# Two dense mixtures of experts in a vision tower: down products in three fp32r parts with tokens along the columns, and router products and convolution taps moved

## The reference, cut to what matters

```python
# f0: every expert on every token, gates from a tree of sigmoids
h = jnp.einsum('nd,edh->neh', flat_x, w1) + b1[None]     # 8 experts, hidden 512
h = jax.nn.gelu(h, approximate=False)
y = jnp.einsum('neh,ehd->ned', h, w2) + b2[None]
out = jnp.einsum('ned,ne->nd', y, leaf_probs)
# f2: the same form, hidden 256, gelu with tanh, gates = the two best of a softmax
# state layer: four taps of a convolution over the tokens, then a scan
yc = sum((conv_w[None, :, k:k + 1] * xp[:, :, k:k + S] for k in range(D_CONV)))
```

## Time and profile before

| | |
|---|---|
| median of the runs | 1373.87 us |
| the profiled execution, its own time | 1372.67 us |
| its span | 1370.9 us |
| PE busy | 1214.8 us (89%) |
| DVE, ACT, POOL busy | 740.2, 749.8, 465.4 us |
| down products, L367, both mixtures | 1728 instructions, 208.4 us busy |
| up products, L352 | 720 instructions, 169.5 us |
| gelus, L380 | 240 instructions, 148.4 us |
| mean granted TensorE clock | 0.933 |

### The profile page before, as it was taken

The page is one execution under the profiler, slowest core; times in us unless marked ns, Lnnn a source line. Parts: engine busy times, 40 slices in busy tenths (PEclk is TensorE's granted clock), DMA queues, the critical chain, the costliest instruction groups (busy, mean ns, idle before and its releaser), DMA issues. The chain is left out here.

```text
span 1370.9 us, 32149 instructions
## 1 busy us (share of the span) xinstructions
PE 1214.8 (89%) x9999; PEld 1041.0 (76%) x9999; DVE 740.2 (54%) x2665; ACT 749.8 (55%) x2598; POOL 465.4 (34%) x844
## 2 busy tenths in 40 slices
PE   8999989999998999868287599998999899868996
PEld 5777779999997888758176477787999687647885
DVE  0588721111115489935655587863332388744774
ACT  1588734444443455427244488864434298743995
POOL 0488730010003268846177243221000011022552
PEclk9999979999999799979599799988999899968998
DMA  6100000010001000000411300000000000023441
GB/s 264 53 2 3 2 1 16 17 32 15 16 0 47 1 1 2 2 16 21 164 47 38 118 1 2 2 2 8 16 15 8 12 2 0 1 72 89 137 139 57
DMA packets 39495, 49.33 MB, mean 36 GB/s; under 512 B 8181, under 2 KB 27492, under 8 KB 39116
## 3 DMA queue, kind: packets, MB, share of 16 engines
q1 hardware_dynamic: 33500, 36.28, 8.6%
q0 software_dynamic: 4176, 6.56, 1.8%
q10 hardware_dynamic: 1696, 4.98, 0.9%
HBM read 41.78 MB, written 6.56 MB: 35 GB/s over the span
## 5 line engine op out<-in xcount | busy, mean ns | idle before, releaser
L380 ACT ACTIVATE f_hid<-quad_bank,f_b1s 128x512 f32<-128x512 f32 (+1 forms) x240 | 148.4, 645 | 176.8 <-PE quad_bank L352 176.5
L470 DVE SCALAR_TENSOR_TENSOR XT<-bank,GATE,XT 128x128 f32<-128x128 f32 x288 | 81.0, 344 | 244.9 <-PE bank L367 244.6
L367 PEld LDWEIGHTS bank<-f_w2s,f_hid 128*128 128x128 f32 x1728 | 206.3, 196 | 3.8
L367 PE MATMUL bank<-f_w2s,f_hid 128*128 128x128 f32 x1728 | 208.4, 279 | 0.0
L352 PE MATMUL quad_bank<-XP,f_w1p 128*128 128x512 f32 (+1 forms) x720 | 169.5, 383 | 0.0
L352 PEld LDWEIGHTS quad_bank<-XP,f_w1p 128*128 128x128 f32 x720 | 125.3, 193 | 21.2
L810 ACT ACTIVATE a_E<-quad_bank,a_shift 108x108 f32<-108x108 f32 x352 | 118.8, 356 | 3.3 <-DVE a_shift L877 2.8
L301 POOL TENSOR_TENSOR f_w1p<-f_w1s,const 128x512 fp32r<-128x512 f32 (+1 forms) x16 | 13.3, 829 | 221.2 <-DMA f_w1s<-in_f_w 221.2
L66 PE MATMUL quad_bank<-const 128*128 128x256 f32 x212 | 62.5, 453 | 15.4 <-PEq L2101 4.5
L810 ACT ACTIVATION_READ_ACCUMULATOR a_E<-quad_bank,a_shift 108x1 f32 x352 | 74.5, 212 | 0.0
L612 POOL TENSOR_TENSOR a_ve<-a_mv,const 108x1 f32<-108x1 f32 x44 | 8.4, 192 | 182.0 <-DVE a_mv L934 181.4
(11 more groups left out here) (455 smaller groups left out, 2959.3 us busy)
## 6 DMA issues: line engine op xcount, KB each, us to landing
a_wqk<-in_a_wqk SPq DMA_DIRECT2D x24, 256.0 KB, 2.6
pats<-in_patches SPq DMA_DIRECT2D x5, 648.0 KB, 10.9
pats<-in_patches ACTq DMA_DIRECT2D x5, 648.0 KB, 12.6
a_wo<-in_a_wo SPq DMA_DIRECT2D x24, 128.0 KB, 2.0
f_w1s<-in_f_w SPq DMA_DIRECT2D x8, 256.0 KB, 2.7
f_w2s<-in_f_w SPq DMA_DIRECT2D x8, 256.0 KB, 3.1
f_w1a<-in_f_w SPq DMA_DIRECT2D x1, 2048.0 KB, 10.4
f_w2a<-in_f_w SPq DMA_DIRECT2D x1, 2048.0 KB, 15.5
```

The lines of the kernel that those rows point to most:

```text
L367: mm = pe.matmul(self.y_bank(n)[:, g * D:(g + 1) * D], self.hid[:, n % 2, c, g * 128:(g + 1) * 128], self.w2s[:, u, c * 128:(c + 1) * 128] ...
L380: act.activation(self.hid[:, n % 2, c, 0:k * 128], self.m.quad_bank[:, i % 4, 0:k * 128], self.func, bias=self.b1s[:, u, c:c + 1]).then_in ...
L470: ins = dve.scalar_tensor_tensor(out=h, in0=y[:, (g - c0) * D:(g - c0 + 1) * D], scalar=m.GATE[:, bass.ds(e + g * 8, 1)], in1=h, op0=ALU.m ...
```

## The change

- `down` has the weights stationary and 512 tokens as columns: per chunk the high and the low weight part times the high hidden part (L458), and after all chunks the high weight part times the low hidden part (L463): 12 fp32r products per block in f0, 6 in f2, with channels on partitions in one bank.
- ACT copies each gelu's f32 result to a high part (`gelu_high`), DVE subtracts for the low part (`lows`). POOL splits the down weights too. In f2 the ups run two blocks ahead (`lead`), in f0 one.
- Gates are turned once (in block 2 of expert 0), stored to DRAM, and for each expert and block loaded again with every partition holding the same row (`repeat`, 256 KB, four buffers). DVE computes (y + b2) * gate (`gated`) and adds (`add`); expert 0's sum is kept raw and multiplied when its gates are there (`raw`, `lazy`). The sums have channels on partitions, so behind the last down only the turning back is left, of which three parts stand between the last downs.
- `route` makes two products per tile, of 16 and 8 columns, one tile per attention step; the best-of-softmax gates come in two pieces behind `raw` of blocks 0 and 1. The loops over experts are written out.
- The taps are loaded early in a0 and made by POOL behind f0's last weight split (`Taps`); the first convolution input is made by ACT and DVE, and PE's first convolutions stand between turns and routes.

```diff
+    def sync(self, sp):
+        sp.dma_start(self.win[:, :], self.io["ss_win"]).then_inc(self.loaded, 16)
+        sp.dma_start(self.raw, self.io["ss_taps"]).then_inc(self.loaded, 16)
...
+    def gpsimd(self, pool):
+        pool.wait_ge(self.loaded, 32)
+        one = self.m.one.broadcast_to([128, 512])
+        for k in range(TAPS):
+            pool.tensor_tensor(self.raw[:, k, :], self.raw[:, k, :], self.win[:, CW:CW + 512], ALU.mult).then_inc(self.steps, 1)
+            pool.wait_ge(self.steps, 2 * k + 1)
+            pool.tensor_tensor(self.wtp[:, 0, k, :], self.raw[:, k, :], one, ALU.mult).then_inc(self.steps, 1)
+            pool.wait_ge(self.steps, 2 * k + 2)
+            pool.tensor_tensor(self.wtp[:, 1, k, :], self.raw[:, k, :], self.wtp[:, 0, k, :], ALU.subtract).then_inc(self.made, 1)
...
+        def repeat(e, n):
+            k = self.gate_at(e, n)
+            if k >= 4:
+                sp.wait_ge(*self.gate_used(k - 4))
+            _, _, t0, w = self.block(e * self.nb + n)
+            sp.dma_start(self.gb[:, k % 4, 0:w], self.g_rows[e:e + 1, t0:t0 + w].broadcast_to([128, w])).then_inc(self.g_loaded[k % 4], 16)
...
+        sp.wait_ge(self.gt_ready, 1)
+        for k in range(2):
+            sp.dma_start(self.g_rows[4 * k:4 * k + 4, :].rearrange("e (t k) -> (e t) k", k=128), self.gT[:, k, :]).then_inc(self.g_stored, 16)
+        sp.wait_ge(self.g_stored, 32)
+        load(2)
+        for n in range(self.nb):
+            repeat(0, n)
+            repeat(1, n)
+        for e in range(2, self.experts):
+            if e + 1 < self.experts:
+                load(e + 1)
+            for n in range(self.nb):
+                repeat(e, n)
...
+    def split_down(self, pool, e):
+        pool.wait_ge(self.w_loaded[1], (e + 1) * 16)
+        if e > 1:
+            pool.wait_ge(self.y_psum, (e - 1) * self.nb)
+        self.split(pool, e, 1)
+    def split(self, pool, e, k):
+        high, low = self.wp[k][:, e % 2, 0, :], self.wp[k][:, e % 2, 1, :]
+        pool.tensor_tensor(high, self.ws[k][:, :], self.m.one.broadcast_to([128, self.chunks * 128]), ALU.mult).then_inc(self.w_high[k], 1)
+        pool.wait_ge(self.w_high[k], e + 1)
+        pool.tensor_tensor(low, self.ws[k][:, :], high, ALU.subtract).then_inc(self.w_split[k], 1)
...
+            out = psum[:, (t - base) * 16:(t - base + 1) * 16]
+            pe.matmul(out, self.xp[:, 0, t * 128:(t + 1) * 128], self.wrp[:, :, :].rearrange("p a e -> p (a e)"), start=True, stop=False,
+                      skip_group_check=True)
+            mm = pe.matmul(out[:, 0:8], self.xp[:, 1, t * 128:(t + 1) * 128], self.wrp[:, 0, :], start=False, stop=True,
+                           skip_group_check=True)
...
+        at_least(pe, self.y_used, i - 1)
+        for c in range(self.chunks):
+            q = i * self.chunks + c
+            pe.wait_ge(self.hid_high, q + 1)
+            for a in range(2):
+                pe.matmul(self.y_bank(i)[:, 0:w], self.wp[1][:, e % 2, a, c * 128:(c + 1) * 128], self.hi[:, q % self.ring, 0:w],
+                          start=(c == 0 and a == 0), stop=False)
+        for c in range(self.chunks):
+            q = i * self.chunks + c
+            pe.wait_ge(self.hid_low, q + 1)
+            mm = pe.matmul(self.y_bank(i)[:, 0:w], self.wp[1][:, e % 2, 0, c * 128:(c + 1) * 128], self.lo[:, q % self.ring, 0:w],
+                           start=False, stop=(c == self.chunks - 1))
+        mm.then_inc(self.y_psum, 1)
...
-        pe.wait_ge(self.hid_ready, e * (self.nb * self.chunks) + (n + 1) * self.chunks)
-        if n == 0:
-            at_least(pe, self.y_used, e * self.nb + 1)
-        elif n > 1:
-            pe.wait_ge(self.y_used, e * self.nb + n)
-        for g in range(k):
-            for c in range(self.chunks):
-                mm = pe.matmul(self.y_bank(n)[:, g * D:(g + 1) * D], self.hid[:, n % 2, c, g * 128:(g + 1) * 128],
-                               self.w2s[:, u, c * 128:(c + 1) * 128], start=(c == 0), stop=(c == self.chunks - 1))
-        mm.then_inc(self.y_psum, 1)
...
+    def gelu_high(self, act, i, c):
+        e, n, t0, w = self.block(i)
+        q = i * self.chunks + c
+        act.wait_ge(self.hid_full, q + 1)
+        at_least(act, self.y_psum, i - self.lead)
+        act.activation(self.hi[:, q % self.ring, 0:w], self.full[:, q % 4, 0:w], ACT.Copy).then_inc(self.hid_high, 1)
+    def hidden(self, act, i):
+        for c in range(self.chunks):
+            self.gelu(act, i, c)
+            if c:
+                self.gelu_high(act, i, c - 1)
+        self.gelu_high(act, i, self.chunks - 1)
...
+    def lows(self, dve, i):
+        e, n, t0, w = self.block(i)
+        for c in range(self.chunks):
+            q = i * self.chunks + c
+            dve.wait_ge(self.hid_high, q + 1)
+            at_least(dve, self.y_psum, i - self.lead)
+            dve.tensor_tensor(self.lo[:, q % self.ring, 0:w], self.full[:, q % 4, 0:w], self.hi[:, q % self.ring, 0:w],
+                              ALU.subtract).then_inc(self.hid_low, 1)
...
+    def lazy(self, dve, n):
+        _, _, t0, w = self.block(n)
+        k = self.take_gates(dve, 0, n)
+        dve.wait_ge(self.y_used, n + 1)
+        x = self.sums[:, t0:t0 + w]
+        dve.tensor_tensor(x, x, self.gb[:, k % 4, 0:w], ALU.mult).then_inc(self.lazied, 1)
+    def gated(self, dve, i):
+        e, n, t0, w = self.block(i)
+        k = self.take_gates(dve, e, n)
+        dve.wait_ge(self.y_psum, i + 1)
+        if i - 2 >= self.nb:
+            dve.wait_ge(self.summed, i - 2 - self.nb + 1)
+        dve.scalar_tensor_tensor(out=self.gated_y[:, i % 2, 0:w], in0=self.y_bank(i)[:, 0:w], scalar=self.b2s[:, e:e + 1],
+                                 in1=self.gb[:, k % 4, 0:w], op0=ALU.add, op1=ALU.mult).then_inc(self.y_used, 1)
+    def add(self, dve, i):
+        e, n, t0, w = self.block(i)
+        dve.wait_ge(self.y_used, i + 1)
+        if e == 1:
+            dve.wait_ge(self.lazied, n + 1)
+        else:
+            dve.wait_ge(self.summed, i - 2 * self.nb + 1)
+        x = self.sums[:, t0:t0 + w]
+        dve.tensor_tensor(x, x, self.gated_y[:, i % 2, 0:w], ALU.add).then_inc(self.summed, 1)
...
+        for i in range(downs, self.last):
+            if ups <= i + self.lead < self.last:
+                self.up(pe, i + self.lead)
+            self.down(pe, i)
+            if i == 2:
+                turn_gates()
+            if i == nb - 1 and self.aside is not None:
+                pe.wait_ge(self.gt_ready, 1)
+                self.aside.tensor(pe)
+            if i > self.last - nb:
+                back(i - (self.last - nb) - 1)
+        for j in range(nb - 1, len(CHUNKS)):
+            back(j)
...
+        for i in range(self.last):
+            e, n = divmod(i, nb)
+            if done <= i + self.lead < self.last:
+                self.lows(dve, i + self.lead)
+            if e == 0:
+                self.raw(dve, n)
+                if n < len(self.gates_last):
+                    self.gates_last[n](dve)
+                if n == len(self.gates_last) - 1:
+                    dve.drain()
+                    dve.tensor_copy(self.gs[:, :, :].rearrange("p e t -> p t e"), m.GATE[:, :].rearrange("p (t e) -> p t e", e=8)).then_inc(self.gs_ready, 1)
+                continue
...
             def after_step(t):
-                if t == G + 2:
-                    mix.route(pe, 0, 8, qkbank[0])
                 if t == G + 3:
-                    mix.route(pe, 8, 14, qkbank[0])
                     pe.wait_ge(exps, 2 * G)
-                    mix.up(pe, 0, 0, 0)
-                if t == G + 4:
-                    mix.up(pe, 0, 0, 1)
+                    pe.wait_ge(mix.lg_ready, 1)
+                    mix.up(pe, 0)
                 if t == G + 5:
-                    mix.route(pe, 14, 16, qkbank[0])
-                    mix.down(pe, 0, 0, 0, 0)
+                    mix.route(pe, early_tiles, 14, qkbank[0], early_tiles)
+                    mix.up(pe, 1)
                 if t == G + 6:
-                    mix.up(pe, 0, 0, 2)
+                    mix.route(pe, 14, 16, qkbank[0], early_tiles)
+                    mix.down(pe, 0)
                 if t == G + 7:
-                    mix.route(pe, 16, NT, qkbank[0])
+                    mix.route(pe, 16, NT, qkbank[0], early_tiles)
             run(pe, step, depth)
             if mix is not None:
-                mix.down(pe, 0, 0, 0, 1)
-                for n in range(3, mix.nb):
-                    mix.up(pe, 0, 0, n)
-                    mix.down(pe, 0, 0, 0, n - 1)
-                mix.down(pe, 0, 0, 0, mix.nb - 1)
-                mix.tensor(pe)
+                mix.tensor(pe, 2, 1)
...
-            keep_busy(pe, m, seg_bank, 10)
-            pe.wait_ge(r_loaded, 16)
-            for n, (c, k) in enumerate(CHUNKS):
-                keep_busy(pe, m, seg_bank, 1)
-                if n:
-                    route(n - 1)
-            route(nb - 1).then_inc(lg_psum, 1)
-            pe.wait_ge(taps_split, 1)
```

(33 more changed lines are left out.)

729 lines of the change are left out of this document (274 added, 455 removed).

## The result

| | before | after |
|---|---|---|
| median of the runs | 1374.04 us | 1312.31 us (1310.78 to 1315.38) |
| the profiled execution | 1372.67 us, span 1370.9 | 1315.38 us, span 1313.6 |
| down products, both mixtures | 208.4 us busy | 178.8 us (L458 115.0, L463 63.8) |

What follows compares the result with a forecast made beforehand. PE was taken to set the pace in f0. Gains of 19.4, 8, 21.8, 7.2 and 8.1 us less a 1.1 loss made 63.4 off the profiled 1372.67: 1309.3, median 1310.5 us, range 1298 to 1332.

Steps and rivals of the forecast that it cites:

- main term: Down blocks in f0 fall from 3.48 to an up block's 2.84 us, giving steady f0's 19.4 us gain.
- page rule: TensorE price: three one-pass parts cost three quarters of f32, 2.61 us a block; total near 1297; rejected for the rows.
- steady f0: f0 from block 3's up in expert 0 to the last down's end: 212.7 to 193.3 us, gain 19.4.
- POOL makes them beside the last two experts: Making the convolution's taps on POOL late in f0, rather than on DVE, was to cost nothing.
- f0's start: Fewer router products and a shorter stretch to block 3's up in f0: gain 8 us, bounds 0 and 12.
- tails: Stretch behind the last down in f0 and f2: gain 10.9 us each, 21.8 in all, bounds 8 and 12 each.
- state phase: From its first statistics to the scan's first transposes: 38.55 to 31.3 us, gain 7.2, bounds 3 and 11.
- f2's start: Gain 5.6 us from routers and clock, loss 6.7 around the gates' turn: net loss 1.1; bounds gain 6, loss 5.
- f2 steady: f2's remaining experts to the last down's end, at 13.0 us each: 100.4 to 92.3 us, gain 8.1.
- first rival: DVE and POOL never overlap, so an f2 expert takes 15.4 us; total 1327 us; chance 0.13.
- The sign that the forecast gave for this rival: DVE's lows and POOL's splits longer than 0.68 and 0.73 us, or PE waiting for low parts in f2.
- second rival: Repeated gates arrive late from DRAM in both mixtures, costing 81 us in all; total 1391 us; chance 0.05.

Runs made afterwards that it cites:

- e5: Changed kernel with both mixtures' down products in true f32 at 512 columns, other engines' work kept; 1361.8 us, ratio 0.9735 to the kernel before.
- e10: e8 with POOL's taps in four pieces behind the splits of experts 2 to 5 instead of one burst; 1301.2 us, ratio 0.9493 to the kernel before.
- e7: Changed kernel with the convolution's taps made by DVE at the state phase's start instead of POOL; 1333.7 us, ratio 0.9540 to the kernel before.
- e2: Changed kernel with POOL's splits of expert 1's weights moved into the attention's steps; 1354.1 us, ratio 0.9575 to the kernel before.
- e8: Changed kernel with expert 1's splits where POOL waits and f2's gates turned behind the fourth down; 1332.0 us, ratio 0.9526 to the kernel before.
- e3: Changed kernel with f0's early up and down products issued sooner, beneath the hand-overs; 1342.1 us, ratio 0.9599 to the kernel before.
- e1: Changed kernel, unedited, run again on another chip; 1349.6 us, ratio 0.9652 to the kernel before.
- e4: Changed kernel with f2's gates turned behind the fourth down block instead of the third; 1333.3 us, ratio 0.9538 to the kernel before.
- e12: Changed kernel, unedited, run beside e9 and e10 on the same chip; 1313.2 us, ratio 0.9589 to the kernel before.
- e6: Changed kernel with the downs' third product (low weights by high hidden values) left out; 1313.0 us, ratio 0.9389 to the kernel before.
- e9: Changed kernel with every load of repeated gates issued twice, the second into unread spare buffers; 1321.1 us, ratio 0.9636 to the kernel before.

## Why the prediction was right, and where its steps were not

**The main term was right in cause and, for a block, in size.** A down block at an up block's price, 2.84, measured 2.80. e5 shows that it is the parts that count: with f32 and 512 columns the block is back at 3.44. The page rule weighed there (the Trainium skill, FP8 and Floating Point Precision, TensorE Precision Notes: four passes for true FP32) would have three parts at three quarters, an estimate; on this chip 2.78 against 3.44 is 0.81, so the rows were the better price.

**That steady f0 gained 18.9 for 19.4 is partly luck.** Up and down take 5.58 us for the forecast's 5.68, so an expert takes 25.05 for 25.7, some 4.5 us less in seven experts. The step "POOL makes them beside the last two experts ...: nothing" was false and took them back: the burst of taps stretches the last two distances to 28.5 and 27.3 us (the last is 25.9 in e10), and costs 4.0 us by e7 and 4.4 by e10.

**f0's start: the term was mis-sized, 8 forecast and 1.7 measured.** From the first up to block 3's the forecast had 24.1 us, the trace has 30.07. First up and output product take 5.4 for 3.9, the stretch from there to the last router product 17.0 for "about 14.5, with the second up and the first down beneath them", the up and down behind it 7.7 for 5.7.

The last of these is explained: 1.9 us are the wait for ACT, of which the forecast had nothing. Expert 1's splits held the low parts up (5.53 us for four), and with them the logits, the gates' table change and the gelus. In e2 and e8, where they don't meet, the start is 2.2 us shorter. The other 4 us lie in the hand-overs, with PE's waits of 2.2 and 4.0 us and the low clock of the second up behind them. It is tempting to blame PE's order, in which the second up stands behind a hand-over; but e3 put it ahead of that, another hand-over got longer, and the start lost 1.6. So the chain through DVE, POOL, PE and ACT is itself longer than forecast, and why stays open.

Another 2 us belong to this one execution: its two slices of 5 us from 55 to 65 us, in the attention, have a granted clock of 0.61 and 0.70, where the kernel before and e1, e4 and e12 have 1.00, and its first up starts at 173.31. In the other traces but e2's it starts at 170.3 to 171.7, and block 3's up in the unedited ones at 200.6 and 200.7: 4.5 us gained of the 8, against the one trace of before.

**The tails** were right (10.8 and 10.6 for 10.9).

**The state phase gained 9.2 for 7.2.** The first convolution came 8.24 in (8.4 forecast). Turns, routers and the second convolution were done 18.7 in for 20.3, which is most of the miss; from there to the first turn it was 10.7 us for 11.0. Here the taps' move paid, but e7 charges nearly all of it to f0.

**f2's start.** Its wait ahead of the gates' turn was forecast at 7.8 and is 5.88 plus 1.09 for the raw sum; the loss from first down to expert 1 was forecast at 6.7 and is 6.7. The gain ahead of it was 3.4 for 5.6, in a stretch that holds the sorted experts too, so where the 2.2 were lost is open. e4 shows that the wait was a matter of place, worth 5.1.

**f2 steady gained 10.9 for 8.1.** The forecast took 13.0 an expert because DVE and ACT looked nearly as long as PE's 12.9; seven experts in 89.5 less 1.3 are 12.6, and an expert in which PE waits for nothing takes 12.52, PE's own price (4.5 times 2.78).

**The first rival was half right.** DVE and POOL do hold each other up: the Trainium skill, SBUF — State Buffer, section Who interferes with whom, has a DVE instruction with two SBUF inputs contend with a GpSimd instruction that reads SBUF. The trace agrees: in f2 low parts of 512 columns take 0.80 us in the mean for 0.68 and the splits 0.81 and 1.19 for 0.73; in f0's burst a low part takes 1.65. The sign that the forecast gave for this rival was thus seen, but not its consequence, 15.4 us an expert. POOL is busy only 21.1 of 75 us there, and two blocks of lead probably cover a held-up low part; no run takes the lead away. In f2 DVE is at its limit all the same (75.00 of 75 us, e6): there the change has used up what PE can give. The better sign was the one that did not come, PE waiting for low parts in f2.

**The second rival** was ruled out by rows with no wait for gates, with less room than assumed (e9).

Misses of +6.3 (f0's start), +2.2 (f2's start), -2.0 (state), -2.8 (f2 steady), +0.9 (steady f0 and tails) and +1.5 behind f2 make the 6.1 us between the forecast gain of 63.4 and the profiled 57.3; the median, 3.1 below the profiled execution, brings the time back to within 1.8 of the forecast. That is closer than the working deserves: stretches missed by 10.9 us one way and 4.8 the other.

## What to carry to other kernels

Price a replaced product by the nearest row with the same operand types, and check what sits behind it: here PE's gain was kept, but in f2 it ended where DVE is busy all the time, and a third fewer down products won only 1.8 us more (e6). Work on POOL is not free beside DVE even when POOL is 40% busy: place it where one of the two waits, or in pieces smaller than DVE's slack (e8 and e10, 7.3 us of f0 with no work removed). When a wait in an engine's order is for a result that nobody else needs soon, move the waiting instruction behind work that is ready (e4).

## What the runs showed of the hardware that was not expected

In e2's trace two small DVE instructions that read one tile each ran until one of POOL's splits ended: a 108x4 `TENSOR_SCALAR` took 1.15 us for 0.17, a 108x256 `COPY` 1.14 for 0.29. The two between them, which lay within the splits as well, took 0.27 and 0.19.

In the same execution the attention's PE, busy 9.6 us and more of every 10 in e4's trace, was busy 8.98 and 8.88 in the two slices with these stalls. The granted clock then went to 0.50 and stayed there for some 17 and 34 us, though PE was busy 9.8 us and more of each 10 again. The other traces have 1.00 from 70 to 160 us. This was seen in one execution, and two others of the same kernel were 25 us shorter, so neither what starts such a stretch nor what ends it is settled.
